# A chain of five attention layers on one core: one layer's PSUM banks rearranged, and one layer's key copy moved from VectorE to ScalarE

## The chip, the core and the metric

One core of a Trainium2 chip runs the whole program. Its engines each run their own instruction queue in order: TensorE (PE in the rows, PEld its weight loads) multiplies and writes PSUM, VectorE (DVE) and ScalarE (ACT) read PSUM and write SBUF, GpSimd (POOL) works on SBUF, SyncE (SP) issues transfers. They wait for each other on semaphores. The metric is the device time of one execution in microseconds; lower is better.

## The reference

Eight residual blocks are applied to `x` (32 items of 128 rows by 128 features) in turn: five of them hold an attention.

```
x = x + L0_xattn(ctx, layernorm(x))      # 16 heads, keys and values straight from ctx
x = x + L0_ffn(layernorm(x))
x = x + L1_xattn(...); x = x + L1_ffn(...)  # 16 heads, 4 gathered tiles only
x = x + L2_xattn(ctx, layernorm(x))      # 8 heads
x = x + L2_ffn(...)
x = x + L3_xattn(ctx, layernorm(x))      # 8 heads, with projections before and after
x = x + L3_ffn(...)                      # L4 below: 16 heads, causal; then experts
attention: softmax(q k^T * scale + bias per key) v, per head and item
L0: keys scaled by 8**-0.5 (0 for an item with no valid key); L3: product with W_out added to x
```

## The kernel before, in words

The program is a list of phases, with a barrier of all engines between two of them. One attention phase (called L0, L1, L2, L3, L4) is written once, as a program for each engine (`attention_vector`, `attention_scalar`, `attention_gpsimd`, `attention_tensor`), and used five times. L0, L2, L3 and L4 handle 32 items, L1 handles 4 tiles.

Each phase is a software pipeline. In one step every engine does one stage for each of up to nine items; `at(lag, stage)` does the stage for the item that entered `lag` steps ago. The order of the lines in `step` is the order of the engine's queue, written by hand. An item passes through these stages:

- lag 1: TensorE transposes the query and key rows into PSUM bank 6 (L775, L776). VectorE copies the query with a mask for the heads (`take_qT`, L386) and the key (`take_kT`, L393 in L0 and L2, L400 in L3) to SBUF.
- lag 2: TensorE makes the raw scores (bias L670, products L677). VectorE takes the negated maximum over the keys (L369 in L0, four of 512 columns; L361 in L3, one of 1024).
- lag 3: GpSimd splits the maximum in two bf16 parts (L485, L486), TensorE transposes them (`turn_max`, L750), ScalarE copies them (`take_nmT`, L532).
- lags 4 and 5: TensorE makes the final scores (L649) and adds the maximum (L687), ScalarE takes the exponential (L550 in L0, L544 in L3), TensorE multiplies with the values (`weighted`, L824), ScalarE copies the result (`take_pv`, L560).
- lag 6: TensorE picks the heads together (the picks, L793). VectorE divides by the sum (`take_o`: L413, L419).
- lags 7 and 8, in L1, L3 and L4 only (`post`): TensorE transposes the result (L768), VectorE copies it (`take_oT`, L404), TensorE multiplies with the output weights (the product, L764), VectorE adds it to the stream (`add_post`, L426) and takes statistics (L264).

TensorE's step is `halves(..., 0)`, `turns`, `halves(..., 1)`, `weighted`. `turns` has a first part (product, transposes), which counts the semaphore `first_turned` when it is done, and a last part (the picks), which counts `last_turned`. In phases with `post` the first part goes first and the transposed maximum belongs to the last part, in bank 7; in L0 and L2 the last part goes first and the maximum belongs to the first part, in bank 6. Whoever writes a PSUM bank waits until the others have read it, by the `done` calls.

Of the kernel before, what the change touches and what calls it, by code (L numbers as in the profile page):

```python
# [24 lines left out]
RING = 4  # L25
# [98 lines left out]
def build(nc, t_in, out):  # L124
    with ExitStack() as ctx_:
# [147 lines left out]

        def turned_max(post):

            return bank_b[7][:, 800:928] if post else bank_b[6][:, 512:640]

        def max_turned(post):

            return "last_turned" if post else "first_turned"  # L280

# [63 lines left out]
        def attention_vector(dve, L, count, heads, normalise, post):  # L345
# [32 lines left out]
            def take_qT(b, k):  # L378
                dve.wait_ge(*after("first_turned", b + 1))
                if not post:  # L380
                    if b < 2:
# [40 lines left out]
            def add_post(b, k):  # L422
                dve.wait_ge(*after("first_turned", b + 8))
                stream = {"L1": x1_tiles, "L3": x_all, "L4": z_all}[L]
                dst = stream[:, b, :]
                nc.vector.tensor_tensor(dst, dst, ps[:, 6, 384:512], ALU.add).then_inc(sem("x_updated"), 1)  # L426
                if count == B:
# [13 lines left out]
            def step(items):  # L441
# [4 lines left out]
                at(2, take_max, 0)  # L446
                if not post:
# [15 lines left out]
        def attention_gpsimd(pool, L, count, heads, raw):  # L463
# [3 lines left out]
            def copy_rows(b, k):  # L467
# [4 lines left out]
                if L in BIASES:  # L472
                    done(pool, max_turned(post), b - 4, count)
                    spots = nm3[:, (k + 2) % RING, :].rearrange("p (g c) -> p g c", g=4)[:, :, 8:11]
# [3 lines left out]
            def split_max(b, k):  # L478
# [4 lines left out]
                pool.wait_ge(*after("max_taken", (b + 1) * raw_jobs(L)))  # L483
                done(pool, max_turned(post), b - 2, count)
                link(nc.gpsimd.tensor_copy(spots[:, :, :, 0], nm))  # L485
# [31 lines left out]
        def attention_scalar(act, L, count, heads, raw, post):  # L517
            dh, per, N = parts_of(heads)

            def norm_q(b, k):  # L520
                if isinstance(b, int) and b == 0:
# [3 lines left out]
                                     scale=inv_all[:, bass.ts(b, 1)]).then_inc(sem("q_row"), 1)  # L525

            def take_nmT(b, k):
                act.wait_ge(*after(max_turned(post), b + 3))
# [3 lines left out]
                nc.scalar.activation(nmT[:, k, :], turned_max(post), ACT.Copy).then_inc(sem("nmT_ready"), 1)  # L532

            def take_first_biases(t, slot):
                act.wait_ge(*after(max_turned(post), t))
                nc.scalar.activation(nmT[:, slot, :], turned_max(post), ACT.Copy).then_inc(sem("early_nmT"), 1)

# [52 lines left out]
        def attention_tensor(pe, L, count, heads, mask_parts, mask, post_w):  # L590
# [34 lines left out]
            def halves(r_item, s_item, u):  # L625
# [6 lines left out]
                if s_item is not None:  # L632
# [6 lines left out]
                    for g in s_groups:  # L639
# [4 lines left out]
                        bank, at = final_at(L, b, g, N)  # L644
                        dst = ps[:, bank, at:at + N]
                        for part in range(mask_parts if masked_scores else 0):
                            nc.tensor.matmul(dst, mask(k, part), identb[:].unsqueeze(1).broadcast_to(four),
                                             start=part == 0, stop=False, skip_group_check=True)
                        nc.tensor.matmul(dst, kT[rows_of(g), k, :], qTm[rows_of(g), k, 0:N],  # L649
                                         start=not masked_scores, stop=False, skip_group_check=True)  # L650
                if r_item is not None:
# [76 lines left out]
            def turns(items):  # L728
# [13 lines left out]
                def turn_max(last):  # L742
# [6 lines left out]
                    slot = item(3)[1] if item(3) else (at_one - 2) % RING  # L749
                    return nc.tensor.transpose(turned_max(post), nm3[:, slot, :], identb[:])  # L750

                def first_part():
                    done(pe, "q_masked", at_one - 1, count)
                    done(pe, "kT_ready", at_one - 1, count)
                    if post:
                        done(pe, "oT_ready", at_one - 7, count)
                        done(pe, "x_updated", at_one - 8, count)
                    else:
                        max_read()
                    last = None  # L760
                    if post and item(8):
                        b, k = item(8)
                        done(pe, "oT_ready", b, count)
                        last = nc.tensor.matmul(ps[:, 6, 384:512], oT[:, k % 2, :], post_w, start=True, stop=True)  # L764
                    if post and item(7):
# [3 lines left out]
                    if item(1):  # L769
# [30 lines left out]

                if post:
                    first_part()
                    last_part()
                else:
                    last_part()
                    first_part()

            def weighted(b, k):
                done(pe, "v_ready", b, count)
                done(pe, "pv_ready", b - 1, count)  # L810
                if post:
                    done(pe, "nmT_ready", b + 2, count)
                done(pe, "o_scaled", b - 1, count)
                ready = "probs_masked" if cut_later else "probs_ready"
# [1493 lines left out]
```

## Time and profile before

| | |
|---|---|
| median of three runs | 1488.82 us (1483.87, 1488.82, 2147.0) |
| profiled execution | 1487.87 us, of it the span of instructions 1486.1 us |
| mean granted TensorE clock | 0.909 |
| TensorE matmul busy | 1319.7 us, 89% |
| TensorE weight load busy | 866.4 us, 58% |
| VectorE busy | 940.0 us, 63% |
| ScalarE busy | 597.2 us, 40% |
| GpSimd busy | 276.5 us, 19% |

The shares are averages over fifteen phases with different limits, so they only say that TensorE works most of the time. Which wait ends last has to be read in the two phases that the change touches: L0 from about 22 to 200 us, and L3 from about 773 to 916 us. A row of the timeline gives the start, the duration, the engine, the line, the operation, and in brackets how long its engine was idle before it and what it had waited for. Durations of neighbours overlap, so the pace of an engine is read from the starts.

### The profile page before, as it was taken

The page shows a single profiled execution, that of the slowest core. Times are in us where ns is not written, and L with a number is a line of the kernel's source. Part 1 is how long each engine was busy: PE and PEld are TensorE (multiplying, and loading weights), DVE is VectorE, ACT ScalarE, POOL GpSimd, SP SyncE. Part 2 cuts the span into 40 slices and gives each one's busy share as a digit, 9 for nine tenths or more (in the row PEclk, how much of TensorE's full clock was granted, in tenths as well). Part 3 has the DMA queues.
Part 4 walks back from the last instruction along what each step waited for, and adds up shares of the span by engine and source line. Part 5 has one row for each costly group of instructions (what it writes and reads, how often), then busy time and mean ns, then how long its engine had stood idle before and what let it go on. Part 6 is the DMA issues. An engine that isn't in the chain of part 4 may idle for free. (4 is left out here: it accounts for less than half of the span.)

```text
span 1486.1 us, 36952 instructions
## 1 busy us (share of the span) xinstructions
PE 1319.7 (89%) x13899; PEld 866.4 (58%) x13899; DVE 940.0 (63%) x2842; ACT 597.2 (40%) x1343; POOL 276.5 (19%) x782
## 2 busy tenths in 40 slices
PE   3999988749759979998998887899999969999998
PEld 2888876535447754444657775336788844444443
DVE  5788759964357768996336776524777754554554
ACT  2777745631326652222433444642444421111111
POOL 0222211300223320000001211322444520000000
PEclk9999998959869989997998998755999989999999
DMA  9400000000000000000000000001000000000000
GB/s 284 119 3 3 4 1 2 2 1 2 1 1 3 3 2 1 1 1 0 1 0 2 2 2 2 1 0 58 3 3 3 3 2 0 15 7 7 7 7 14
DMA packets 26389, 21.30 MB, mean 14 GB/s; under 512 B 5936, under 2 KB 22512, under 8 KB 26224
## 3 DMA queue, kind: packets, MB, share of 16 engines
q1 hardware_dynamic: 25216, 18.87, 4.4%
q8 instruction: 112, 1.84, 0.5%
q14 instruction: 53, 0.43, 0.1%
q10 hardware_dynamic: 1008, 0.16, 0.1%
HBM read 16.93 MB, written 2.10 MB: 13 GB/s over the span
## 5 line engine op out<-in xcount | busy, mean ns | idle before, releaser
L649 PE MATMUL ps<-qTm,kT 32*128 32x512 f32 (+1 forms) x1056 | 266.0, 551 | 2.0 <-ACT probs L554 1.7
L677 PE MATMUL ps<-kT,qTm 32*128 32x128 f32 x3200 | 249.1, 291 | 0.7 <-DVE kT L400 0.6
L677 PEld LDWEIGHTS ps<-kT,qTm 32*128 32x128 f32 x3200 | 224.7, 202 | 6.2 <-issue 2.8
L1897 PE MATMUL ps<-kv_all,ctx_all 128*128 128x512 f32 x256 | 134.2, 606 | 5.2 <-DVE kv_all L1810 5.2
L824 PE MATMUL ps<-probs,v_wide 128*32 128x128 f32 x3200 | 115.6, 277 | 21.8 <-DVE o_sb L419 17.9
L1875 PE MATMUL ps<-q_all,ctx_all 128*128 128x512 f32 x256 | 132.4, 600 | 0.0
L374 DVE TENSOR_REDUCE neg_max<-ps 128x8 f32<-128x1024 f32 x72 | 87.7, 1218 | 70.5 <-PE ps L677 70.4
L1834 ACT ACTIVATE kv_all<-ps,b_col 128x512 f32<-128x512 f32 x64 | 44.0, 687 | 216.1 <-PE ps L1875 216.1
L554 ACT ACTIVATE probs<-ps 128x1024 f32<-128x1024 f32 x72 | 73.7, 1024 | 128.5 <-PE ps L687 128.5
L1810 DVE TENSOR_SCALAR kv_all<-ps,b_col 128x512 f32<-128x512 f32 x64 | 48.0, 750 | 116.6 <-PE ps L1875 116.6
L649 PEld LDWEIGHTS ps<-qTm,kT 32*128 32x128 f32 x1056 | 89.1, 188 | 54.4 <-issue 44.6
L485 POOL CAST nm<-neg_max 128x16 bf16<-128x16 f32 (+1 forms) x132 | 26.9, 204 | 444.6 <-DVE neg_max L361 173.2
L386 DVE TENSOR_TENSOR qTm<-ps,hmask 128x512 f32<-128x512 f32 (+1 forms) x132 | 73.4, 556 | 51.0 <-PE ps L776 29.3
L824 PEld LDWEIGHTS ps<-probs,v_wide 128*32 128x32 f32 x3200 | 81.7, 110 | 38.7 <-issue 31.1
L369 DVE TENSOR_REDUCE neg_max<-ps 128x4 f32<-128x512 f32 x128 | 82.1, 683 | 32.0 <-PE ps L677 32.0
L687 PE MATMUL ps<-nmT,sel_max 32*128 32x128 bf16 x1600 | 98.9, 218 | 0.0
L550 ACT ACTIVATE probs<-ps,bias_col 128x512 f32<-128x512 f32 x128 | 80.9, 683 | 43.3 <-PE ps L687 43.3
L1493 PE MATMUL ps<-tap_w,xqT 128*128 128x512 f32 x192 | 93.6, 624 | 0.0
L560 ACT ACTIVATE pv<-ps 128x256 f32<-128x256 f32 x132 | 50.6, 383 | 87.1 <-PE ps L824 84.1
L1875 PEld LDWEIGHTS ps<-q_all,ctx_all 128*128 128x128 f32 x256 | 49.1, 192 | 61.3 <-issue 61.3
L793 PE MATMUL ps<-pv_pick,pv 128*128 128x72 f32 (+1 forms) x528 | 83.9, 281 | 0.9 <-ACT pv L560 0.6
L544 ACT ACTIVATE probs<-ps,bias_col 128x1024 f32<-128x1024 f32 x64 | 71.3, 1114 | 31.9 <-PE ps L687 31.9
(376 smaller groups left out, 2693.1 us busy)
## 6 DMA issues: line engine op xcount, KB each, us to landing
ctx_all<-in_ctx SPq DMA_DIRECT2D x4, 1024.0 KB, 11.3
x_all<-in_x SPq DMA_DIRECT2D x4, 512.0 KB, 7.3
out<-x_all SPq DMA_DIRECT2D x8, 256.0 KB, 2.3
ctx_all<-in_W1T SPq DMA_DIRECT2D x1, 1024.0 KB, 5.1
tap_w<-in_conv_wT SPq DMA_DIRECT2D x1, 768.0 KB, 7.1
w_l<-in_w SPq DMA_DIRECT2D x2, 256.0 KB, 3.4
above<-in_c_above SPq DMA_DIRECT2D x1, 256.0 KB, 3.1
rope<-in_c_rope SPq DMA_DIRECT2D x1, 256.0 KB, 2.7
```

Of the source, the lines that this page charges most:

```text
L369: nc.vector.tensor_reduce(neg_max[:, k, per * g:per * g + per], ps[:, raw_bank(L, b, g), 0:N].rearrange("p (h k) -> p h k", h=per), AX.X, ...
L374: nc.vector.tensor_reduce(neg_max[:, k, H2 * u:H2 * u + H2].rearrange("p (a h) -> p a h", a=2), ps[:, 4 * u:4 * u + 2, 0:N].rearrange("p a ...
L550: nc.scalar.activation(probs[:, k % 2, N * g:N * (g + 1)], ps[:, final_bank(L, b, g), 0:N], ACT.Exp, bias=bias).then_inc(sem("probs_ready" ...
L554: nc.scalar.activation(probs[:, k % 2, 2 * N * u:2 * N * (u + 1)].rearrange("p (a n) -> p a n", a=2), ps[:, 2:4, 0:N], ACT.Exp, bias=bias) ...
L649: nc.tensor.matmul(dst, kT[rows_of(g), k, :], qTm[rows_of(g), k, 0:N], start=not masked_scores, stop=False, skip_group_check=True)
L677: last = nc.tensor.matmul(dst, qTm[rows_of(g), k, 128 * i:128 * i + 128], kT[rows_of(g), k, :], start=False, stop=True, skip_group_check=True)
L687: last = nc.tensor.matmul(dst, sel_max[rows_of(g), i, :], nmT[rows_of(g), k, :], start=False, stop=True, skip_group_check=True)
L793: last = nc.tensor.matmul(ps[:, 7, 256 + W * half:256 + W * half + W], pv[:, k % 2, 128 * half:128 * half + 128], pv_pick[:, 0 if heads == ...
L824: last = nc.tensor.matmul(ps[32 * j:32 * j + 32, 7, 128 * half:128 * half + 128], v_tile(k % 2, heads, 4 * half + j, i), probs[:, k % 2, 1 ...
L1493: last = nc.tensor.matmul(dst, xqT[:, k % 2, tap:tap + 128], tap_w[:, tap, :], start=False, stop=tap == 2)
L1875: nc.tensor.matmul(ps[:, c % 2, :], w_up[:, c, :], xm_T[:, k, :], start=True, stop=True).then_inc(sem("mo_hidden"), 1)
L1897: nc.tensor.matmul(ps[:, 4 + e % 2, :], w_down[:, c, :], hid[:, c % 4, :], start=c % 4 == 0, stop=c % 4 == 3).then_inc(sem("mo_down"), 1)
```

## The change

In L3 the parts of `turns` are reordered as they are in L0 and L2: the last part (now product and picks) goes first, the first part (transposes, now with the transposed maximum) second. The transposed maximum moves from bank 7 to bank 6, the product from bank 6 to bank 7. VectorE does `take_o` and `add_post` ahead of the copies of query, key and result. In L0 the scaled copy of the turned keys is issued by ScalarE, between the exponentials and the copy of the maximum. In phases with masked scores the masks of both groups now come before both products; this concerns L1 alone.

```
+        LOW = ("L0", "L2") + ("L3",)
+        def turned_max(L):
+            return bank_b[7][:, 800:928] if L not in LOW else bank_b[6][:, 512:640] if L in ("L0", "L2") else bank_b[6][:, 768:896]
+        def max_turned(L):
+            return "first_turned" if L in LOW else "last_turned"
+        def product_at(L):
+            return ps[:, 7, 0:128] if L in LOW else ps[:, 6, 384:512]
...
             def take_oT(b, k):
                 dve.wait_ge(*after("first_turned", b + 7))
+                if L in LOW:
+                    done(dve, "nmT_ready", b + 7 - 3, count)
...
             def add_post(b, k):
-                dve.wait_ge(*after("first_turned", b + 8))
+                dve.wait_ge(*after("last_turned" if L in LOW else "first_turned", b + 8))
...
                 at(2, take_max, 0)
-                if not post:
+                if L in LOW:
                     at(6, take_o)
+                    if post:
+                        at(8, add_post)
                 at(1, take_qT)
-                at(1, take_kT)
+                if L != "L0":
+                    at(1, take_kT)
                 if post:
                     at(7, take_oT)
+                if L not in LOW:
                     at(6, take_o)
-                if post:
+                if L not in LOW:
                     at(8, add_post)
...
+            def take_keys(b, k):
+                act.wait_ge(*after("first_turned", b + 1))
+                done(act, "scores", b - RING, count, final_jobs(L))
+                nc.scalar.activation(kT[:, k, :], ps[:, 6, 128:256], ACT.Copy, scale=k_scale[:, 0, bass.ts(b, 1)]
+                                     ).then_inc(sem("kT_ready"), 1)
...
                 at(5 if final_jobs(L) == 1 else 4, exps, 1)
+                if L == "L0":
+                    at(1, take_keys)
...
                 at(3, take_nmT)
...
                 def first_part():
...
-                    if raw:
+                    if L in LOW:
                         last = turn_max(last)
...
                 def last_part():
-                    if post:
+                    if L not in LOW:
                         max_read()
+                    elif post:
+                        done(pe, "x_updated", at_one - 8, count)
                     done(pe, "o_scaled", at_one - 6, count)
                     done(pe, "pv_ready", at_one - 5, count)
-                    last = turn_max(None) if post else None
+                    last = turn_max(None) if L not in LOW else product() if post else None
...
-                if post:
+                if L not in LOW:
                     first_part()
                     last_part()
                 else:
...
             def weighted(b, k):
...
-                if post:
+                if L not in LOW:
                     done(pe, "nmT_ready", b + 2, count)
+                elif post:
+                    done(pe, "x_updated", b - 3, count)
```

TensorE in one full step of L3, from the product to the next, before:

```order
L764 MATMUL ps<-w_out,oT 128x128
L768 MATMUL ps<-ident,o_sb 128x128
L775 MATMUL ps<-ident,q_all 128x128
L776 MATMUL ps<-ident,kv_all 128x128
L750 MATMUL ps<-identb,nm 128x128
L793 MATMUL ps<-pv_pick,pv 128x68 x2
L649 MATMUL ps<-qTm,kT 128x256 x2
L670 MATMUL ps<-nmT,sel_bias 128x256 x2
L677 MATMUL ps<-kT,qTm 128x128 x4
L687 MATMUL ps<-nmT,sel_max 128x128 x4
L824 MATMUL ps<-probs,v_wide 32x128 x8
```

and now:

```order
L783 MATMUL ps<-w_out,oT 128x128
L827 MATMUL ps<-pv_pick,pv 128x68 x2
L800 MATMUL ps<-ident,o_sb 128x128
L807 MATMUL ps<-ident,q_all 128x128
L808 MATMUL ps<-ident,kv_all 128x128
L776 MATMUL ps<-identb,nm 128x128
L671 MATMUL ps<-qTm,kT 128x256 x2
L696 MATMUL ps<-nmT,sel_bias 128x256 x2
L703 MATMUL ps<-kT,qTm 128x128 x4
L713 MATMUL ps<-nmT,sel_max 128x128 x4
L860 MATMUL ps<-probs,v_wide 32x128 x8
```

The picks moved ahead of the four transposes; nothing was added or removed. VectorE in one full step of L3, before:

```order
L386 TENSOR_TENSOR qTm<-ps,hmask 128x256
L400 COPY kT<-ps 128x128
L404 COPY oT<-ps 128x128
L413 RECIPROCAL inv_den<-ps 128x8
L419 TENSOR_TENSOR o_sb<-ps,inv_den 128x128
L426 TENSOR_TENSOR x_all<-x_all,ps 128x128
L264 BN_STATS stats_all<-x_all 128x6
L361 TENSOR_REDUCE neg_max<-ps 128x8
```

and now:

```order
L423 RECIPROCAL inv_den<-ps 128x8
L429 TENSOR_TENSOR o_sb<-ps,inv_den 128x128
L436 TENSOR_TENSOR x_all<-x_all,ps 128x128
L264 BN_STATS stats_all<-x_all 128x6
L394 TENSOR_TENSOR qTm<-ps,hmask 128x256
L408 COPY kT<-ps 128x128
L414 COPY oT<-ps 128x128
L367 TENSOR_REDUCE neg_max<-ps 128x8
```

Four operations that ended the queue's step ahead of the maximum now begin it. ScalarE in one full step of L0, before:

```order
L532 ACTIVATE nmT<-ps 128x128
L524 ACTIVATE row<-x_all,shift_all,inv_all 128x128
L550 ACTIVATE probs<-ps,bias_col 128x512 x2
L560 ACTIVATE pv<-ps 128x256
L567 ACTIVATE q_all,ctx_sq<-ctx_all 128x256
```

and now:

```order
L544 ACTIVATE kT<-ps,k_scale 128x128
L552 ACTIVATE nmT<-ps 128x128
L538 ACTIVATE row<-x_all,shift_all,inv_all 128x128
L570 ACTIVATE probs<-ps,bias_col 128x512 x2
L580 ACTIVATE pv<-ps 128x256
L587 ACTIVATE q_all,ctx_sq<-ctx_all 128x256
```

One operation came to this queue, behind a pair of exponentials and ahead of the copy of the maximum; on VectorE the row L393 is gone from L0's step.

## Rows read from the trace of the kernel before

**Rows 1.** Busy us of PE, PEld, DVE, ACT, POOL; then clock, DMA, GB/s: L0, L3

```profile
53.00:182.00 129.00, 128.93 (x2671) 111.90 (x2665) 106.66 (x241) 99.39 (x239) 33.23 (x138) 1.00 0.06 15
797.90:893.06 95.16, 83.91 (x1490) 67.68 (x1488) 70.27 (x192) 42.59 (x72) 18.05 (x95) 1.00 0.01 2
```

**Rows 2.** Waits (us in total, times, longest): L3's full steps, then all L3

```profile
PE ps L824 <- DVE o_sb L419: 11.2, 24, 0.6
...
PE ps L824 <- DVE o_sb L419: 14.6, 30, 0.8
```

**Rows 3.** Timeline of TensorE, one step of L3, and one later row

```profile
844.01 0.64 PE L824 MATMUL ps<-probs,v_wide 128*32 128x128 f32 x16 [0.46 <-DVE o_sb L419]
844.59 0.48 PE L649 MATMUL ps<-qTm,kT 32*128 32x256 f32 x2
...
845.33 0.49 PE L764 MATMUL ps<-w_out,oT 128*128 128x128 f32 x2
845.65 0.27 PE L768 MATMUL ps<-ident,o_sb 128*128 128x128 f32 x1
...
845.87 0.27 PE L776 MATMUL ps<-ident,kv_all 128*128 128x128 f32 x1
846.11 0.22 PE L750 MATMUL ps<-identb,nm 128*128 128x128 bf16 x1
846.16 0.61 PE L793 MATMUL ps<-pv_pick,pv 128*128 128x68 f32 x4
...
897.80 0.22 PE L750 MATMUL ps<-identb,nm 128*128 128x128 bf16 x1 [0.18 <-POOL nm L486]
```

**Rows 4.** Timeline of VectorE, the same step of L3

```profile
842.21 0.42 DVE L386 TENSOR_TENSOR qTm<-ps,hmask 128x256 f32<-128x256 f32 x1 [0.78 <-PE ps L776]
842.55 0.28 DVE L400 COPY kT<-ps 128x128 f32<-128x128 f32 x1
842.75 0.28 DVE L404 COPY oT<-ps 128x128 f32<-128x128 f32 x1
843.22 0.21 DVE L413 RECIPROCAL inv_den<-ps 128x8 f32<-128x8 f32 x1 [0.19 <-ACT nmT L532]
843.46 0.29 DVE L419 TENSOR_TENSOR o_sb<-ps,inv_den 128x128 f32<-128x128 f32 x1
843.67 0.28 DVE L426 TENSOR_TENSOR x_all<-x_all,ps 128x128 f32<-128x128 f32 x1
...
844.19 1.21 DVE L361 TENSOR_REDUCE neg_max<-ps 128x8 f32<-128x1024 f32 x1
```

**Rows 5.** Timeline of L2, whose parts already stand in the new order

```profile
497.44 0.22 PE L750 MATMUL ps<-identb,nm 128*128 128x128 bf16 x1
497.59 0.48 PE L649 MATMUL ps<-qTm,kT 32*128 32x256 f32 x2
...
497.73 0.27 ACT L532 ACTIVATE nmT<-ps 128x128 bf16<-128x128 bf16 x1
...
498.09 0.43 DVE L386 TENSOR_TENSOR qTm<-ps,hmask 128x256 f32<-128x256 f32 x1 [0.34 <-ACT nmT L532]
...
498.33 0.64 PE L824 MATMUL ps<-probs,v_wide 128*32 128x128 f32 x16
```

**Rows 6.** Timeline of L0, one step: ScalarE, VectorE, TensorE

```profile
103.64 0.28 ACT L532 ACTIVATE nmT<-ps 128x128 bf16<-128x128 bf16 x1
...
104.82 1.26 ACT L550 ACTIVATE probs<-ps,bias_col 128x512 f32<-128x512 f32 x2 [0.52 <-PE ps L687]
...
104.06 0.68 DVE L386 TENSOR_TENSOR qTm<-ps,hmask 128x512 f32<-128x512 f32 x1
...
104.92 1.28 DVE L369 TENSOR_REDUCE neg_max<-ps 128x4 f32<-128x512 f32 x2
...
105.77 0.39 PE L670 MATMUL ps<-nmT,sel_bias 32*128 32x512 bf16 x2
```

**Rows 7.** One line of ScalarE: a copy scaled by a column (ns min/median/max)

```profile
L1537 ACT ACTIVATE q_all<-ps,mask_q x32: 359/367/368, 696.0 to 773.2; 128x128 f32<-128x128 f32 x32
```

More of the change, by code:

```diff
@@ L379, in take_qT @@
                 dve.wait_ge(*after("first_turned", b + 1))
-                if not post:
-                    if b < 2:
+                if L in LOW:
+                    if b < 2 and L not in BIASES:
+                        pass
+                    elif b < 2:
                         dve.wait_ge(*after("early_nmT", b + 1))
@@ L472, in copy_rows @@
                 if L in BIASES:
-                    done(pool, max_turned(post), b - 4, count)
+                    done(pool, max_turned(L), b - 4, count)
                     spots = nm3[:, (k + 2) % RING, :].rearrange("p (g c) -> p g c", g=4)[:, :, 8:11]
@@ L483, in split_max @@
                 pool.wait_ge(*after("max_taken", (b + 1) * raw_jobs(L)))
-                done(pool, max_turned(post), b - 2, count)
+                done(pool, max_turned(L), b - 2, count)
                 link(nc.gpsimd.tensor_copy(spots[:, :, :, 0], nm))
@@ L525, in norm_q @@
                                      scale=inv_all[:, bass.ts(b, 1)]).then_inc(sem("q_row"), 1)
+            def take_keys(b, k):
[3 more added lines that the diff above has]
+                                     ).then_inc(sem("kT_ready"), 1)
             def take_nmT(b, k):
-                act.wait_ge(*after(max_turned(post), b + 3))
+                act.wait_ge(*after(max_turned(L), b + 3))
                 done(act, "scores", b - RING, count, max(final_jobs(L), 2))
@@ L644, in halves @@
                         bank, at = final_at(L, b, g, N)
-                        dst = ps[:, bank, at:at + N]
                         for part in range(mask_parts if masked_scores else 0):
-                            nc.tensor.matmul(dst, mask(k, part), identb[:].unsqueeze(1).broadcast_to(four),
+                            nc.tensor.matmul(ps[:, bank, at:at + N], mask(k, part), identb[:].unsqueeze(1).broadcast_to(four),
                                              start=part == 0, stop=False, skip_group_check=True)
-                        nc.tensor.matmul(dst, kT[rows_of(g), k, :], qTm[rows_of(g), k, 0:N],
-                                         start=not masked_scores, stop=False, skip_group_check=True)
+                        if not masked_scores:
+                            nc.tensor.matmul(ps[:, bank, at:at + N], kT[rows_of(g), k, :], qTm[rows_of(g), k, 0:N],
+                                             start=True, stop=False, skip_group_check=True)
+                    for g in s_groups if masked_scores else ():
+                        bank, at = final_at(L, b, g, N)
+                        nc.tensor.matmul(ps[:, bank, at:at + N], kT[rows_of(g), k, :], qTm[rows_of(g), k, 0:N],
+                                         start=False, stop=False, skip_group_check=True)
                 if r_item is not None:
@@ L749, in turn_max, with product @@
                     slot = item(3)[1] if item(3) else (at_one - 2) % RING
-                    return nc.tensor.transpose(turned_max(post), nm3[:, slot, :], identb[:])
+                    return nc.tensor.transpose(turned_max(L), nm3[:, slot, :], identb[:])
+                def product():
+                    if not item(8):
+                        return None
+                    b, k = item(8)
+                    done(pe, "oT_ready", b, count)
+                    return nc.tensor.matmul(product_at(L), oT[:, k % 2, :], post_w, start=True, stop=True)
                 def first_part():
@@ L756, in first_part @@
                         done(pe, "oT_ready", at_one - 7, count)
+                    if L in LOW:
+                        max_read()
+                    elif post:
                         done(pe, "x_updated", at_one - 8, count)
-                    else:
-                        max_read()
                     last = None
[L761 to L764, printed above, removed]
+                    if post and L not in LOW:
+                        last = product()
                     if post and item(7):
@@ L776, in first_part @@
                         last = nc.tensor.transpose(ps[:, 6, 128:256], key_rows(b), ident[:])
-                    if raw:
+                    if L in LOW:
                         last = turn_max(last)
@@ L810, in weighted @@
                 done(pe, "pv_ready", b - 1, count)
-                if post:
+                if L not in LOW:
                     done(pe, "nmT_ready", b + 2, count)
+                elif post:
+                    done(pe, "x_updated", b - 3, count)
                 done(pe, "o_scaled", b - 1, count)
```

13 lines of the change are left out of this document (4 added, 9 removed).

## The prediction

> **What bounds the kernel now.** I read the busy time by stretch first, since the change touches two phases only. In L0's full steps TensorE is busy 128.93 of 129.00 us, VectorE 106.66, ScalarE 99.39; in L3's full steps TensorE has 83.91 of 95.16 us and VectorE 70.27 [rows 1]. So L0 is paced by TensorE, and in L3 TensorE is idle for 11 us although it has work. The waits say for what: `weighted` (L824) waits for VectorE's scaled result (L419), 24 times in the stretch of 95.16 us, 11.2 us in all, and 30 times, 14.6 us, in all of L3 [rows 2]. That gives 24 full steps of 95.16 / 24 = 3.97 us.
>
> The timelines show why. VectorE can begin a step of L3 only when the keys are transposed (L776 ends at 845.87 + 0.27 = 846.14, and L386 starts 0.04 later, one step after 842.21), because the copies of query, key and result stand ahead of the reciprocal [rows 3, 4]. The reciprocal starts 1.01 us after L386 (843.22 against 842.21), and the result is ready at 843.46 + 0.29 = 843.75; 0.26 later TensorE starts L824 [rows 3, 4]. Meanwhile TensorE had only half a step of scores to do. This is a loop of one step: L824, half a step, product, transposes, five VectorE operations, L824. In it TensorE idles 0.46 us, and before the transposed maximum (L750) another 0.13: L750 follows L776 by 0.24 us instead of the 0.11 between neighbouring transposes (845.65 to 845.87 are two of them) [rows 3]. That second wait is for GpSimd's split of the maximum, as a row of the drain names it [rows 3]. Without both, TensorE's own step is 3.97 - 0.46 - 0.13 = 3.38 us.
>
> **The change in L3.** Nothing is added or taken away; two things move.
>
> The picks go ahead of the transposes and `take_o` to the head of VectorE's step, so the loop that cost 0.46 is opened: from the product at T the picks start 0.32 later (845.33 to 845.65 is what a product occupies), last 0.61, and the reciprocal starts 0.04 after, at T + 0.97 [rows 3, 4]. The result is ready at 0.97 + 0.24 + 0.29 = T + 1.50, on TensorE 0.26 later, T + 1.76. L824 is due at T + 0.32 + 0.61 + 0.33 for three transposes, so L750 at T + 1.26 at the latest, then + 0.15 + 0.74 by L2's rows, T + 2.15 [rows 5]. So this wait goes entirely.
>
> What is late next is the key. It now stands behind four operations: reciprocal to result 0.24, to the addition 0.21, to the end of the statistics 0.52, query 0.34, and its own 0.28, in sum 1.59 [rows 4]. So it is ready at 0.97 + 1.59 = T + 2.56. The raw scores of the next half step need it, 0.26 later, T + 2.82, and from there to the next product is 0.74 (844.59 to 845.33) [rows 3]. This new loop of one step makes 3.56 us.
>
> Two other waits are new. The copies of query and key now wait for the transposed maximum and for ScalarE's copy of it, 0.65 us from L750 to L386 as L2 shows [rows 5]: T + 1.26 + 0.65 = T + 1.91, against T + 1.94 when VectorE comes there. Hidden, just. And the maximum starts at T + 1.94 + 0.34 + 0.20 + 0.20 = T + 2.68 and ends 1.21 later; from there to L750 is 846.11 - 845.40 = 0.71 [rows 3, 4], so L750 can start at T + 4.60, and it is due 1.26 to 1.13 after the next product (picks at full length or not), so this asks for a step of 3.34 to 3.47, also below 3.56. The product waits in addition for ScalarE's copy of the previous result and for the last addition (queued behind it: the picks and all transposes), and `weighted` for this step's addition, ready at T + 0.97 + 0.24 + 0.21 + 0.28 + 0.26 = T + 1.96 against T + 2.15; they cost nothing while L824 is not early by 0.19.
>
> The step is thus between TensorE's own 3.38 and the loop's 3.56. I take 3.50, nearer the loop, because its 0.61 for the picks is a modelled end. Gain: 24 x (3.97 - 3.50) = 11.3 us, at the ends 24 x 0.59 = 14.2 and 24 x 0.41 = 9.8. Outside the full steps the same wait cost 14.6 - 11.2 = 3.4 us in six steps [rows 2]; in the last ones no query or key stands in VectorE's way, in the first ones the transposed maximum now holds the query back. I take 2.0 of it (0 to 3.4).
>
> **The change in L0.** VectorE's key copy leaves: the step from L386 to L369 is 0.86 us now, 0.60 of it the query (0.68 less the 0.08 by which neighbours overlap), 0.26 the key [rows 4, 6]. ScalarE gets a copy of the same size scaled by a column, 0.37 us [rows 7], ahead of `take_nmT`. The next pair of exponentials is covered: ScalarE idles 0.52 before it [rows 6], 0.15 are left. What is not covered is the query's copy, which waits for `take_nmT`: 103.64 + 0.37 + 0.28 + 0.09 (as from 498.00 to 498.09 in L2) = 104.38 instead of 104.06 [rows 5, 6]. So L369 comes at 104.38 + 0.60 = 104.98, against 104.92 before; with the copy overlapped by 0.10, at 104.88. The relief of 0.26 and the delay of 0.32 cancel. Behind it, TensorE's L670 at 105.77 needs a bank that the first of the two maxima frees (104.92 + 0.64 + 0.26 = 105.82 for the second of its two matmuls) [rows 6]: no slack. Price: -0 (TensorE is full) to +0.06 x 28 = +1.7 us. I take +0.3, for the first steps, where the copy delays the first query and nothing hides it.
>
> The Trainium skill (Perfetto Trace Analysis, Identifying the Most-Contended Engine) says that matmul busy time does not tell how near TensorE is to its limit and that the share of weight loads does. By it L0 is at 111.90 / 129.00 = 87%, with room that the matmul row hides; if VectorE were what holds it there, the relief would count (rival A).
>
> **L1, ends and clock.** In L1 a product moves past three masks, in four tiles: both ends within 1 us, taken as zero. The clock is granted in full in both stretches [rows 1]; what follows starts some 13 us sooner and may meet the clock's changes otherwise. The undisturbed runs differ by 5 us, so I allow 3 either way.
>
> **Sum.** -11.3 - 2.0 + 0.3 = -13.0. The profiled execution took 1487.87 us, 0.95 under the median; from the median 1488.82 - 13.0 = 1475.8, and I say 1476.
>
> **The rivals.**
>
> - A, more than that: L3 reaches TensorE's own step (-14.2 - 3.4) and in L0 VectorE was the hidden pace, so the step loses 0.26 x 28 = 7.3. Sum -25: 1464. For it: L369's bank comes with no slack. Against: TensorE's 128.93 of 129.00 in L0. The page named above speaks for it. Chance 0.12.
> - B, half of it: VectorE's operations run one after the other at their full lengths in the new loop (0.21 + 0.29 + 0.28 + 0.29 + 0.42 + 0.28 + 0.03 + 0.03 = 1.83 for 1.59), which makes 3.80; 24 x 0.17 = 4 and 1 outside, L0 costs 1.7. Sum -3.5: 1485. For it: the addition's result is waited for before the statistics. Against: the rows overlap. Chance 0.15.
> - C, slower: the loops of L3 close into one. If the picks come late (they wait for the last addition and ScalarE's copy), the reciprocal starts only after L750, and its group of 0.97 joins the chain maximum, GpSimd, L750, ScalarE's copy, query, key, result, maximum: 0.71 + 0.65 + 0.34 + 0.20 + 0.20 + 1.21 = 3.31, with it 4.28 us. Then 24 x 0.31 = +7.4, with L0's 1.7 and no gain outside 1498. It decides from the point where the picks end over 0.3 us later than T + 0.93; slower than before it is from 3.97, 0.41 behind the loop above. Against: L2 keeps this order, and its chain closes without the group. Chance 0.08.
> - The forecast, 1471 to 1481: 0.62. The remaining 0.03 is for what I don't see.
>
> **Numbers.** The likeliest is 1476. The forecast's own range is 1471 to 1481 (9.8 to 14.2, 0 to 3.4, 0 to 1.7, and part of the clock's 3). To hold 8 in 10 it takes in most of A and B: 1465 to 1487; half of A, a third of B and C are left out. A measurement of this kernel can tell about 2% from no change, that is 1459 and 1519. Faster than that needs A and the clock: 0.04. Slower needs C and more, such as a phase at a lower clock: 0.03. Within 2%: 0.93.
>
> **What would show it.** In L3: the wait of L824 for the result gone; a step of 3.4 to 3.56 us from product to product; TensorE's new idle time, 0.05 to 0.2, in front of the raw scores' L696 with the key (L408) as what came last; the reciprocal 0.9 to 1.0 after the product; phase L3 shorter by 11 to 15 us. In L0: a step as long as before, VectorE with 0.26 less per step, ScalarE's idle before the exponentials at 0.15 to 0.25 instead of 0.52, L394 waiting for L552. Wrong it would be by a step of L3 over 3.7 with L824 or L783 waiting, by L750's successor (L776) waiting for GpSimd over 0.2 in each step, or by L0's step changed by more than 0.1.

## The result, and the profile after

The changed kernel takes 1463.53 us (median; 1458.66 to 1465.44), the kernel before, beside it, 1487.8: a ratio of 0.9841, interval 0.9802 to 0.9879. That is 24.3 us less where 13.0 were forecast, and just under the range's low end of 1465. One of the four executions of the kernel before took 2147.0 us and is left out of the ratio; without it that kernel's median is 1486.78 and the difference 23.3. The profiled execution took 1465.44 us with a span of 1463.7, against 1487.87 and 1486.1, so 22.4 us are to be found in the traces.

The busy time by stretch finds them. Columns: the stretch, its length, busy us of PE, PEld, DVE, ACT and POOL, the granted clock, the share and GB/s of the DMA. The stretches are L0 with its feed-forward, L1 and L3. Before:

```profile
21.10:227.30 206.20, 195.17 (x3347) 164.66 (x3347) 150.29 (x378) 134.12 (x337) 42.43 (x171) 0.99 0.17 47
334.20:398.30 64.10, 59.55 (x560) 30.80 (x560) 25.95 (x66) 12.73 (x19) 3.12 (x12) 0.94 0.01 1
773.70:914.90 141.20, 121.34 (x1986) 96.06 (x1986) 94.15 (x254) 59.66 (x101) 24.62 (x128) 0.94 0.01 2
```

and after:

```profile
20.80:227.90 207.10, 195.62 (x3347) 165.15 (x3347) 144.72 (x347) 142.63 (x369) 42.56 (x171) 0.99 0.17 46
333.50:389.50 56.00, 51.24 (x560) 29.20 (x560) 25.75 (x65) 12.64 (x19) 3.12 (x12) 0.92 0.01 2
763.90:890.90 127.00, 120.28 (x1986) 95.20 (x1986) 91.45 (x254) 59.55 (x101) 24.67 (x128) 0.92 0.01 3
```

L3 gave 14.2 us (the forecast had 13.3 for it), L0 took 0.9 (0.3), and L1, which the forecast had at zero, gave 8.1. All the rest together is 1 us (L4 203.2 before, 203.5 after, both at 0.94). L0's 0.9 is less than its stretch varies by itself: in seven other profiled executions, of the changed kernel and of versions of it that leave L0 alone, it took 206.2 to 209.7.

**L1.** The timeline of TensorE shows where. One half of a step of L1 without raw scores, before: three masks (L647) for the first group of heads, its products (L649), three masks for the second group, its products, the maximum (L687), the transposes.

```profile
370.74 0.81 PE L647 MATMUL ps<-identb,kv_all 128*128 128x512 bf16 x3 [0.20 <-ACT probs L554]
371.48 1.12 PE L649 MATMUL ps<-qTm,kT 32*128 32x512 f32 x2
372.53 0.82 PE L647 MATMUL ps<-identb,kv_all 128*128 128x512 bf16 x3
373.28 0.69 PE L649 MATMUL ps<-qTm,kT 32*128 32x512 f32 x1
...
373.81 0.59 PE L649 MATMUL ps<-qTm,kT 32*128 32x512 f32 x1
...
374.56 0.23 PE L750 MATMUL ps<-identb,nm 128*128 128x128 bf16 x1
```

The same half after (the product is L675, the masks L668):

```profile
366.52 1.46 PE L668 MATMUL ps<-identb,kv_all 128*128 128x512 bf16 x6 [0.21 <-ACT probs L574]
367.90 1.13 PE L675 MATMUL ps<-qTm,kT 32*128 32x512 f32 x4
...
369.19 0.23 PE L776 MATMUL ps<-identb,nm 128*128 128x128 bf16 x1
```

The half takes 374.56 - 370.74 = 3.82 us before and 369.19 - 366.52 = 2.67 after. By their starts the masks cost nearly the same (0.74 + 0.75 before, 1.38 for six after, 0.11 less). But two matmuls of the product (one group) take 1.12 us, and all four together, when nothing stands between the groups, 1.13. Each group uses its own 32 rows of the array (32*128 in the row), and the two groups run beside each other. Before, the next masks start 1.05 us after the first group's product (371.48 to 372.53), and from the second group's product to the transposed maximum there are 1.28 us (373.28 to 374.56). After, nearly the same 1.29 us (367.90 to 369.19) hold both groups. So 1.05 of the 1.15 us are the first group's product standing alone, and the rest is the masks. The reading is that a mask, which takes all 128 rows (128*128 in the row), can run beside neither group. It fits the halves with raw scores, where matmuls on 32 other rows do run beside the product (in the changed kernel L675 starts at 351.53 and L703 at 351.54), but no run put a matmul of another kind between the groups. Four items with two halves each, times 1.15 us, are 9.2; the stretch of L1 as a whole became 8.1 shorter.

**L3.** The waits of the 24 full steps, 788.89 to 870.21:

```profile
POOL nm L499 <- DVE neg_max L367: 60.8, 24, 2.8
...
DVE inv_den L423 <- PE ps L827: 11.3, 24, 0.6
```

TensorE's wait for the result [rows 2] is gone; VectorE now waits for the picks. One step, TensorE (L783 is the product, its start is the forecast's T) and VectorE together:

```profile
819.25 0.46 PE L783 MATMUL ps<-w_out,oT 128*128 128x128 f32 x2
...
820.14 0.21 DVE L423 RECIPROCAL inv_den<-ps 128x8 f32<-128x8 f32 x1 [0.45 <-PE ps L827]
820.16 0.27 PE L808 MATMUL ps<-ident,kv_all 128*128 128x128 f32 x1
...
820.40 0.22 PE L776 MATMUL ps<-identb,nm 128*128 128x128 bf16 x1
...
821.44 0.28 DVE L408 COPY kT<-ps 128x128 f32<-128x128 f32 x1
...
821.83 1.21 DVE L367 TENSOR_REDUCE neg_max<-ps 128x8 f32<-128x1024 f32 x1
...
821.88 0.28 PE L696 MATMUL ps<-nmT,sel_bias 32*128 32x256 bf16 x2
...
822.64 0.46 PE L783 MATMUL ps<-w_out,oT 128*128 128x128 f32 x2
```

From 788.89 to 870.21 there are 24 steps, so one takes 3.39 us (3.97 before). The reciprocal comes at T + 0.89 instead of the T + 0.97 of the forecast, the key is ready at 821.72 = T + 2.47 (forecast T + 2.56), and L696 starts 0.16 later, so the way to TensorE is at most 0.16 here, where the forecast had 0.26. L776 follows L808 by 0.24, double its share (0.11 between neighbours in L0, 98.61 to 98.72): it still waits for GpSimd's split of the maximum.

**L0.** One step after, ScalarE, VectorE and TensorE, answering to [rows 6]:

```profile
98.50 0.27 PE L807 MATMUL ps<-ident,row 128*128 128x128 f32 x1
...
98.72 0.22 PE L776 MATMUL ps<-identb,nm 128*128 128x128 bf16 x1
...
99.42 0.37 ACT L544 ACTIVATE kT<-ps,k_scale 128x128 f32<-128x128 f32 x1
...
100.05 0.69 DVE L394 TENSOR_TENSOR qTm<-ps,hmask 128x512 f32<-128x512 f32 x1
...
100.60 1.27 ACT L570 ACTIVATE probs<-ps,bias_col 128x512 f32<-128x512 f32 x2 [0.26 <-PE ps L713]
100.66 1.28 DVE L375 TENSOR_REDUCE neg_max<-ps 128x4 f32<-128x512 f32 x2
...
101.33 0.70 PE L671 MATMUL ps<-qTm,kT 32*128 32x512 f32 x2
101.55 0.39 PE L696 MATMUL ps<-nmT,sel_bias 32*128 32x512 bf16 x2
...
103.27 0.27 PE L807 MATMUL ps<-ident,row 128*128 128x128 f32 x1
```

The step is 103.27 - 98.50 = 4.77 us, as before, the copy takes 0.37, and ScalarE's idle time before the exponentials fell from 0.52 to 0.26.

### The profile page after: what moved, and what is told of

Its sections match the earlier page's. It is cut to its first block and busy times, and to the rows that moved or that the text cites. A ratio compares the mean times of both kernels' runs of the same rounds, so it can differ in the third digit from the quotient of the medians.

```text
span 1463.7 us, 37014 instructions
## 1 busy us (share of the span) xinstructions
PE 1306.9 (89%) x13899; PEld 861.5 (59%) x13899; DVE 932.4 (64%) x2810; ACT 605.9 (41%) x1375; POOL 277.2 (19%) x782
## 5 line engine op out<-in xcount | busy, mean ns | idle before, releaser
L703 PE MATMUL ps<-kT,qTm 32*128 32x128 f32 x3200 | 250.9, 291 | 1.2 <-issue 0.6
L671 PE MATMUL ps<-qTm,kT 32*128 32x512 f32 (+1 forms) x1024 | 249.1, 550 | 1.8 <-ACT probs L574 1.4
L703 PEld LDWEIGHTS ps<-kT,qTm 32*128 32x128 f32 x3200 | 226.1, 202 | 6.9 <-issue 4.2
L860 PE MATMUL ps<-probs,v_wide 128*32 128x128 f32 x3200 | 115.2, 277 | 8.5 <-DVE o_sb L429 3.7
L671 PEld LDWEIGHTS ps<-qTm,kT 32*128 32x128 f32 x1024 | 85.2, 189 | 47.9 <-issue 38.8
L713 PE MATMUL ps<-nmT,sel_max 32*128 32x128 bf16 x1600 | 95.6, 218 | 0.0
L860 PEld LDWEIGHTS ps<-probs,v_wide 128*32 128x32 f32 x3200 | 80.7, 109 | 24.3 <-issue 13.9
```

The source lines that it names most:

```text
L671: nc.tensor.matmul(ps[:, bank, at:at + N], kT[rows_of(g), k, :], qTm[rows_of(g), k, 0:N], start=True, stop=False, skip_group_check=True)
L703: last = nc.tensor.matmul(dst, qTm[rows_of(g), k, 128 * i:128 * i + 128], kT[rows_of(g), k, :], start=False, stop=True, skip_group_check=True)
L713: last = nc.tensor.matmul(dst, sel_max[rows_of(g), i, :], nmT[rows_of(g), k, :], start=False, stop=True, skip_group_check=True)
L860: last = nc.tensor.matmul(ps[32 * j:32 * j + 32, 7, 128 * half:128 * half + 128], v_tile(k % 2, heads, 4 * half + j, i), probs[:, k % 2, 1 ...
```

## The experiments

**The three parts, each alone on the kernel before.** The kernel before took 1488.99 us beside them (31 runs).

*The masks alone:*

```
+                        if not masked_scores:
                             nc.tensor.matmul(... kT[rows_of(g), k, :], qTm[rows_of(g), k, 0:N], ...)
+                    for g in s_groups if masked_scores else ():
+                        nc.tensor.matmul(... kT[rows_of(g), k, :], qTm[rows_of(g), k, 0:N], ...)
```

> The kernel before, with one edit: in the halves of L1's final scores the masks of both row groups come ahead of both key-query products. Theory M (the two products, which use different rows of the array, run beside each other once no full-array mask stands between them): a half of L1 from the masks to the transposes takes 2.7 us instead of 3.8, L1 from its first transpose to its last product is 8 to 10 us shorter, 1477 to 1480 us in all. Rival M0 (the edit is neutral, as the prediction had it, and L1 came out shorter in the changed kernel because the clock rose at another moment): L1 within 1.5 us of before, 1486 to 1489.

Measured: 1478.56 us, ratio 0.9915 [0.9881, 0.9949]. L1 takes 55.6 us instead of 64.1 and L3 141.3. So the order of masks and products is worth 8.5 us in the trace and 10.4 at the medians, as theory M had it, and M0 is out.

*L3's rearrangement alone* (all of the change that hangs on `LOW`):

> The kernel before, with L3's banks and order of parts rearranged alone. Theory B (TensorE reaches its own step of 3.38 us): the step from product to product 3.35 to 3.41, L3 14 us shorter, L1 and L0 as before, 1472 to 1475 us. Rival B0 (the prediction's loop through the key copy): a step of 3.50 to 3.56, 10 to 12 us shorter, 1476 to 1479.

Measured: 1484.61 us, ratio 0.9968 [0.9941, 0.9994], above the range of either theory. In the trace L3 does as theory B says: the step is 3.39 us (24 steps from 809.74 to 891.18), and L3 takes 128.5 us, 12.7 less than before. But the profiled execution took 1493.15 us, because L1 and L4, which are untouched here, took 76.3 and 209.4 instead of 64.1 and 203.2. A second profile below shows more of that.

*L0's key copy alone:*

```
-                at(1, take_kT)
+                if L != "L0":
+                    at(1, take_kT)          # VectorE
+                if L == "L0":
+                    at(1, take_keys)        # ScalarE
```

> The kernel before, with L0's key copy moved to ScalarE alone. Theory K (L0 is paced by TensorE; VectorE's 0.26 us less and its wait for a later copy of the maximum cancel): L0's step 4.77 us as before, first query 0.3 us later, total within 1 us of before. Rival K1 (the move gives part of what the sum did not explain): L0 shorter by 3 us or more, 1484 or less.

Measured: 1487.75 us, ratio 0.9982 [0.9961, 1.0002]: neutral, and L0's step is 4.77 us, as theory K had it.

At the medians the three parts alone give 10.4 + 4.4 + 1.2 = 16.0 us, 7 to 8 less than all of them together. In the traces the two that matter give 8.5 in L1 and 12.7 in L3; with L3's edit alone the profiled execution gave that back in phases that the edit does not touch.

**Is it that products stand side by side?** The changed kernel, with one of the second group's masks put back between the two products. No instruction is added.

```
+                            if g == s_groups[1] and part == mask_parts - 1:
+                                continue
...
+                        if g == s_groups[1]:
+                            nc.tensor.matmul(... mask(k, mask_parts - 1) ...)
                         nc.tensor.matmul(... kT[rows_of(g), k, :], qTm[rows_of(g), k, 0:N] ...)
```

> The changed kernel with one of the masks' matmuls moved: in L1's halves the last mask part of the second group now stands between the two products; same instructions. Theory M (products run beside each other only when adjacent): each half is longer again by 0.9 to 1.2 us, eight halves, so 7 to 10 us slower than the changed kernel, 1471 to 1474 us. Rival M1 (what costs in the old order is that a product follows its own group's last mask in the same bank): only one of the two products does here, so half of it comes back, 4 to 5 us, 1467 to 1469.

Measured: 1485.76 us, ratio 0.9947 [0.9913, 0.9982], of 12 runs three at 1472 to 1475. A half of L1, at the full clock:

```profile
349.90 1.25 PE L670 MATMUL ps<-identb,kv_all 128*128 128x512 bf16 x5
351.08 1.12 PE L680 MATMUL ps<-qTm,kT 32*128 32x512 f32 x2
352.14 0.39 PE L678 MATMUL ps<-identb,kv_all 128*128 128x512 bf16 x1
352.46 0.69 PE L680 MATMUL ps<-qTm,kT 32*128 32x512 f32 x1
...
353.73 0.33 PE L812 MATMUL ps<-ident,kv_all 128*128 128x128 f32 x1
```

One mask in between brings the whole price back: 353.73 - 349.90 = 3.83 us, where the same half of the changed kernel takes 2.68 (350.13 to 352.81). Rival M1 asked for half of that, so it is out. Eight halves explain some 9 us of this run, and its three fastest executions, with a mean granted clock of 0.911 to 0.913, lie 9 to 11 above the changed kernel. The median lies 12 us over the forecast of 1471 to 1474. The seven slowest executions have a clock of 0.898 to 0.901; in the profiled one of them L1 took 74.9 us at 0.76, so the rest goes with the granted clock, most of it in L1's second part, as in the kernel with L3's rearrangement alone.

**The clock in L1.** The changed kernel once more, and L3's rearrangement alone once more; the kernel before took 1486.65 us beside them and beside the next two.

> The changed kernel once more, unchanged, beside the versions below. Question: does its second part of L1 ever run at a low granted clock, as the profiled executions of two other versions did (0.75 over L1 instead of 0.92)? Theory S, the clock's fall belongs to L1's halves in which masks and products alternate: this kernel has none, so its profile shows L1 at 0.92 and 56 us again, and all its executions lie within 1458 to 1468 us. Rival S1, the fall comes by chance and in any version: a part of its executions lies 10 us or more above the rest.

> The kernel before with L3's rearrangement alone (masks and products of L1 alternate as before), one more look. Theory S, L1's alternating halves go with a fall of the granted clock in L1's second part: L1 some 75 us at 0.75 once more. Rival S1, the fall comes by chance: L1 at 0.92 to 0.94 and 64 to 65 us, as in the kernel before's own profile; then L3's 12.7 us are all that differ and the execution takes some 1474 us.

The changed kernel: 1464.16 us, ratio 0.9857 [0.9829, 0.9884], runs from 1461.54 to 1468.69, L1 54.9 us. L3's rearrangement alone: 1474.82 us, one run. Its L1 in the first profile (1493.15 us), up to 375 us and behind it:

```profile
330.10:375.00 44.90, 44.09 (x393) 22.24 (x394) 19.12 (x39) 7.33 (x12) 2.82 (x11) 0.90 0.01 1
375.00:406.40 31.40, 28.52 (x167) 13.94 (x166) 6.61 (x26) 5.51 (x7) 0.30 (x1) 0.55 0.00 1
```

and in this one:

```profile
330.30:375.00 44.70, 43.66 (x440) 22.26 (x441) 19.12 (x39) 8.65 (x14) 3.12 (x12) 1.00 0.01 2
375.00:391.10 16.10, 12.58 (x121) 6.71 (x119) 6.66 (x26) 4.06 (x5) 0.00 (x0) 1.00 0.00 1
```

Same program, same order in L1: 76.3 us with most of the second part at 1.2 GHz (a granted clock of 0.55), 60.8 us at 2.4 GHz throughout. So the fall of the clock does not belong to the alternating order as such, and theory S, in the form that L1 would run low once more, is wrong. That the changed kernel ran as theory S said is then no proof of S. The 1474.82 us lie 12 us under the median of before, near L3's gain of 12.7, and that nearness is in part chance: beside the profile of before L1 took 3.3 us less here, and L4, also untouched, 5.9 more (209.1 at 0.91). In the twelve executions before it L3's gain shows only in part (4.4 us at the medians); the profiled one of them lost 12.2 us in L1 and 6.2 in L4.

**What paces L0?** The changed kernel with the key copy issued twice.

```
+                nc.scalar.activation(row_copy[:], ps[:, 6, 128:256], ACT.Copy, scale=k_scale[...])
                 nc.scalar.activation(kT[:, k, :], ps[:, 6, 128:256], ACT.Copy, scale=k_scale[...])
```

> The changed kernel, but ScalarE issues L0's scaled copy of the keys twice (the second into a row that nobody reads), so the price of the added operation is doubled. Theory K, the copy lies in ScalarE's idle time before the exponentials (0.26 us left of 0.52) and TensorE paces L0: L0's step stays 4.77 us, the time within 1.7 us of the changed kernel. Rival K1, the query's copy follows ScalarE's copy of the maximum without slack, so it comes some 0.26 us later, with it the maximum and TensorE's next step: 0.26 x 28 = +7.3 us, VectorE's L394 waiting for L552 ahead of a late L369.

Measured: 1472.62 us, ratio 0.9895 [0.9873, 0.9916], against 1464.16: 8.5 us more, L0 with its feed-forward 214.0 us. Rival K1 has the mechanism, with 0.19 us a step where it said 0.26. One step:

```profile
98.82 0.69 DVE L395 TENSOR_TENSOR qTm<-ps,hmask 128x512 f32<-128x512 f32 x1 [0.38 <-ACT nmT L554]
99.43 1.28 DVE L376 TENSOR_REDUCE neg_max<-ps 128x4 f32<-128x512 f32 x2
...
99.85 0.70 PE L673 MATMUL ps<-qTm,kT 32*128 32x512 f32 x2
100.26 0.39 PE L698 MATMUL ps<-nmT,sel_bias 32*128 32x512 bf16 x2
```

The query waits 0.38 us for ScalarE's copy of the maximum, and L698, which needs the bank that L376 frees, starts 0.41 behind L673 instead of 0.22 (101.33 to 101.55 above). The step grows by that 0.19, to 4.96 us; times 28 it is 5.3 of the 6.9 to 7.8 us by which the phase grew.

That does not make this chain the pace of the changed kernel. From the query's transpose to the maximum there are 2.21 us before (102.71 to 104.92), 2.16 in the changed kernel (98.50 to 100.66) and 2.42 with the copy doubled (97.01 to 99.43), and the step is 4.77, 4.77 and 4.96. The 0.05 between the first two change nothing, and of the 0.26 between the last two 0.19 arrive in the step. So the chain lay some 0.07 us below what sets 4.77, and what that is, TensorE's own work or another chain, stays open. The busy time does not decide it, since this row has TensorE busy all the time in the step of 4.96:

```profile
53.00:182.00 129.00, 129.00 (x2578) 110.78 (x2580) 99.40 (x208) 111.00 (x287) 32.27 (x134) 1.00 0.05 12
```

**What paces L3?** The changed kernel with L3's statistics behind the maximum.

```
-                    measure(dve, after("x_updated"), b, stream)      # L3, behind the addition
+                if L == "L3":
+                    at(8, lambda b, k: measure(dve, after("x_updated"), b))   # behind take_max
```

> The changed kernel, but in L3 VectorE takes the statistics (L264) after the maximum instead of ahead of the copies of query and key, so the key is ready some 0.2 us sooner in a step. Theory T, L3's step of 3.39 us is TensorE's own work, and the loop through VectorE's copies (3.33 us) ends just below it: no change, within 1 us. Rival T1, that loop still sets the step: 3.39 goes toward 3.2, 24 x 0.2 = -4.8 us.

Measured: 1466.02 us, ratio 0.9862 [0.9844, 0.988]; L3 takes 122.9 us instead of 127.0. Theory T falls, and 4.1 us is near rival T1's 4.8. One step, TensorE:

```profile
818.06 0.46 PE L786 MATMUL ps<-w_out,oT 128*128 128x128 f32 x2
...
818.97 0.27 PE L811 MATMUL ps<-ident,kv_all 128*128 128x128 f32 x1
...
819.09 0.22 PE L779 MATMUL ps<-identb,nm 128*128 128x128 bf16 x1
...
821.33 0.46 PE L786 MATMUL ps<-w_out,oT 128*128 128x128 f32 x2
```

The transposed maximum (L779) now follows the key's transpose by 0.12 instead of 0.24, and from it to the next product TensorE takes 2.24 us in both kernels (819.09 to 821.33; 820.40 to 822.64). The edit moves the key and the maximum alike, but a late key would show behind L776, and nothing changed there. So the key was in time, T1's loop is not the one, and what L3's step of 3.39 us still waited for is the maximum's loop: VectorE's row, the maximum, GpSimd, L776. Without it 23 steps from 798.25 to 874.04 take 3.30 each. At the time of the whole nothing is seen of L3's 4 us: L4 behind it took 205.8 us at a clock of 0.93 (203.5 at 0.94), and two other stretches 2.6 more, one of them ahead of L3. L4 took 205.9 in the kernel with the copy doubled too, so this is not shown to come of the shorter L3.

**The arrangement elsewhere.** L4, and L1, added to the list of phases in the new arrangement; the kernel before took 1488.7 us beside them.

```
-        LOW = ("L0", "L2") + ("L3",)
+        LOW = ("L0", "L2") + ("L3", "L4")        # and in the other kernel ("L3", "L1")
```

> The changed kernel with L4 in the new arrangement as well (product and picks first, the maximum in bank 6). Question: is the arrangement a gain by itself, or only where TensorE waits for VectorE's result? Theory W, only there: in 150 us of L4 in the changed kernel's trace TensorE is busy 146.2 and has no wait for the result (L429), so L4 stays within 2 us of 203.5 and the time of 1464. Rival W1, L4's step shortens as L3's did toward TensorE's bare work: up to 3.8 x 203 / 150 = 5 us less. Rival W2, L4's maximum is longer (two reductions) and its exponentials wait for TensorE 73 us in 150; the later maximum adds to that and L4 grows by 3 us or more.

> The changed kernel with L1 in the new arrangement as well. L1 has four items, so its steps are few and mostly ramp. Theory W, the arrangement frees a loop that only full steps have: L1 within 1 us of 56. Rival W3, in a ramp the picks ahead of the transposes give the last items' results sooner: L1 1 to 3 us shorter, the time 1461 to 1463. Rival W4, the query's copy now waits for the transposed maximum, which a ramp has late: L1 1 to 3 us longer.

L4: 1460.63 us, ratio 0.9794 [0.9754, 0.9835], L4 198.0 us instead of 203.5. Rival W1 has the size. A step of L4 takes 5.45 us (1064.58 to 1070.03) instead of 5.69 (1060.98 to 1066.67). The waits list none for the result in these steps, which is why I expected nothing. The timeline of the changed kernel has the dependence all the same:

```profile
1063.49 0.29 DVE L429 TENSOR_TENSOR o_sb<-ps,inv_den 128x128 f32<-128x128 f32 x1
...
1063.53 0.39 PE L713 MATMUL ps<-nmT,sel_max 32*128 32x128 bf16 x8
1064.04 1.08 PE L860 MATMUL ps<-probs,v_wide 128*32 128x128 f32 x32
```

and the one with L4 rearranged:

```profile
1066.11 0.29 DVE L429 TENSOR_TENSOR o_sb<-ps,inv_den 128x128 f32<-128x128 f32 x1
...
1067.08 0.39 PE L713 MATMUL ps<-nmT,sel_max 32*128 32x128 bf16 x8
1067.40 1.08 PE L860 MATMUL ps<-probs,v_wide 128*32 128x128 f32 x32
```

`weighted` starts 0.26 behind the result (1063.78) in the first, as it did in L3 [rows 3, 4], and 0.51 behind L713; in the second the result has long been there and it is 0.32. It looks like L3's loop once more, 0.19 of the 0.24 us a step. The row of the matmuls before (L713, 1063.53 + 0.39) ends only 0.12 before L860, which may be why the waits do not list it.

L1: 1467.88 us, ratio 0.9851 [0.9812, 0.989], L1 57.6 us at 0.89: no gain. It is 1.6 us more than in the changed kernel's profile, the size of rival W4, but the clock was lower too (0.92 there), so W4 is not shown.

**Together.** L4 in the new arrangement and L3's statistics moved; then L4's statistics moved too. The kernel before took 1486.7 us beside them.

> The changed kernel with L4 in the new arrangement and with L3's statistics behind the maximum: the two edits that shortened a phase, together. Theory P, the phases add: L3 123 us instead of 127, L4 198 instead of 203.5, the time 1464 - 4 - 5.5 = 1454 to 1456. Rival P1, phases that lie behind an earlier end run at a lower granted clock, as L4 did with the statistics moved (205.8 us at 0.93 for 203.5 at 0.94): L3's 4 us are given back, and the time is 1460.

> The same with L4's statistics behind its second maximum as well. Theory Q, in L4 VectorE's copies are not what TensorE waits for (busy 111 of 150 us, TensorE 146): within 1 us of the kernel without it. Rival Q1, L4's copies bind there as they did in L3: 26 x 0.1 = 2.6 us less.

1459.78 us, ratio 0.9814 [0.98, 0.9827], and 1458.41, ratio 0.9809 [0.9793, 0.9825]. Theory P's 1454 to 1456 was not reached. L3 kept its 4 us (123.2), so P1's first half is wrong, but the time is P1's 1460: L4 (200.2 at 0.93, with its edit alone 198.0 at 0.94) took 2.2 more than with L4's edit alone, the stretch between L3 and L4 1.1 and L2 with what follows it 1.6. L2 runs ahead of L3 and cannot owe its part to L3's earlier end. Where that comes from is open. Moving L4's statistics changed L4 by 0.7. These two and L4's edit alone are the fastest and cannot be told apart (1458 to 1461, intervals overlap).

## Why the prediction was wrong

- **The step that failed** is "In L1 a product moves past three masks, in four tiles: both ends within 1 us, taken as zero". The number of instructions was the same and nobody waited, so I priced a reorder at nothing and did not look at what runs beside what on TensorE. The trace of before had it: two matmuls of the product 1.12 us long, then a mask. The runs show 8.1 us in the stretch of L1 (9.2 by eight halves of 1.15), 8.5 in the trace and 10.4 at the medians with this part alone, and all of a half's 1.15 back with one mask between the products. With it the sum is -13.0 - 9.2 = -22.2, or 1466.6, three above the measurement. The Trainium skill (TensorE: Matmul & The Clock Gate, Part 3: Packing small matmuls — row/col tiling) says that matmuls on different rows of the array run concurrently, and I did not apply it here. The trace agrees for neighbours (four in 1.13 us), and adds that one mask over all rows between them ends it.
- **L3's term was too small, mostly right in kind.** Forecast 24 x (3.97 - 3.50) = 11.3, measured 24 x (3.97 - 3.39) = 13.9; outside the full steps 2.0 against 14.2 - 13.9 = 0.3. The wait of L824 left, the reciprocal came at T + 0.89, the gain of the full steps was inside its own ends (9.8 to 14.2). What I chose was wrong: the key's loop (3.56) was laid out with 0.26 for the way to TensorE and 0.97 up to the reciprocal, and measured at most 0.16 and 0.89. The maximum's loop, which I had at 3.34 to 3.47 and set aside as below the key's, is the one that closes: the maximum ends at 821.83 + 1.21, L776 can follow 0.71 later as forecast, and with the maximum 0.2 earlier in VectorE's queue the step fell to 3.30. TensorE's "own step" of 3.38 was no floor either; 3.30 was reached.
- **L0 was right in its number, and of its reasons one nearly holds and one is open.** The relief and the delay cancelled: step 4.77, the copy alone neutral. "No slack" was nearly right: some 0.07 us were left, and doubling the copy costs 0.19 a step. But "TensorE is full" does not follow from 128.93 of 129.00 [rows 1], since the row shows 129.00 in a step 0.19 longer. Here the Trainium skill (Perfetto Trace Analysis, Identifying the Most-Contended Engine) was right that matmul busy time says little. Its other measure, 110.78 / 129.00 = 86% of weight loads in the longer step and 87% before, does not tell the two apart either. VectorE was not the hidden pace, as rival A had it: its maximum came 0.05 earlier and the step stayed.
- **Rival A** has the time (1464) by luck and not by its mechanism: L3's full steps came to its end of them (13.9 of 14.2), but outside them there were 0.3 of its 3.4, L0 gave nothing of its 7.3, and L1, which it did not have, gave 8.1. **B** fell (no step of 3.80), and **C** (slower): the picks were done by T + 0.89 and the loops stayed apart.

## What to carry to other kernels

A reorder on TensorE is not free because its instructions are the same: list for each matmul which rows of the array it uses, and where a full-array matmul stands between two that use different rows and could run side by side, price it at the length of one of them (here 1.05 of 1.15 us). In a loop of several engines, price every closed chain and take the longest by its own rows, also the one that seemed 0.1 below. And test "this engine is full" by adding work elsewhere and seeing how much of it arrives in the step: here overlapping matmul records showed 129.00 of 129.00 us in a step that was 0.19 us longer than it had to be.

## What the runs showed of the hardware

- Two pairs of fp32 matmuls of 32 x 512 on different rows of the array take 1.13 us together and 1.12 us for one pair alone. With a mask of all 128 rows between them the whole is 1.15 us longer (3.83 for 2.68 in L1's halves).
- The granted clock in L1 is not fixed by the kernel: 0.75 and 1.00 over L1 in two executions of one program, 15.5 us apart. These two ran on different chips, but twelve executions on one chip (one mask between the products) also differ by 17 us, with mean clocks of 0.898 to 0.913. A pair of the product that took 1.12 us at 2.4 GHz takes 2.07 at 1.2:

```profile
381.45 2.07 PE L668 MATMUL ps<-qTm,kT 32*128 32x512 f32 x2
```

  The kernels with the products side by side were not seen to do this (8 runs of the changed one within 1458.66 to 1468.69, 8 with the masks alone within 1470.56 to 1479.47). Those with the alternating order spread wider in part (13 of L3's rearrangement alone 1474.82 to 1493.15, 31 of before 1480.57 to 1503.21, but 12 with the key copy alone only 1481.08 to 1489.37). Whether the order makes the fall likelier stays open.
- L4 with unchanged code took 203.1 to 209.4 us in eleven profiled executions, at granted clocks of 0.94 to 0.90. It was 205.8 behind an L3 that was 4 us shorter and 205.9 behind an L0 that was 7 us longer, so neither direction is shown to be the cause. A gain of a few us in one phase has to be read in that phase, since the whole time of one execution can hide it.
